# Layer-1 attention of a two-layer transformer kernel: where sums, inverses, additions and minima stand

## The reference

```python
xn = layer_norm(x, ln_gamma, ln_beta)
q, k, v = heads(xn @ Wq), heads(xn @ Wk), heads(xn @ Wv)
att = jnp.einsum('bhid,bhjd->bhij', q, k) / DIM_HEAD ** 0.5
att = att + alibi_bias(S, N_HEADS)[None]
p = jax.nn.softmax(att, axis=-1)
out = jnp.einsum('bhij,bhjd->bhid', p, v)
out = out.transpose(0, 2, 1, 3).reshape(B, S, INNER)
return out @ Wo
```

## Time and profile before

| what | value |
|---|---|
| median of 3 runs | 2318.41 us (2315.52 to 2321.29) |
| profiled execution, its own time | 2305.89 us |
| its span | 2304.0 us |
| granted TensorE clock, mean | 0.985 |
| TensorE, VectorE, GpSimd, ScalarE busy | 95%, 79%, 1385.3 us (60%), 1234.0 us (54%) |
| layer-1 attention | its maxima (line 1034) start from 372.4 to 1906.4 us |

### The profile page before, as it was taken

How to read it: one execution, slowest core, us unless ns; L and a number is a source line. 1 busy time by engine, 2 the same in 40 slices (tenths; PEclk the granted TensorE clock), 3 DMA queues, 4 the chain that set the end, 5 groups by cost and what they waited for, 6 DMA issues and landing times. The chain is left out here.

```text
span 2304.0 us, 40435 instructions
## 1 busy us (share of the span) xinstructions
PE 2197.2 (95%) x10494; PEld 1381.0 (60%) x10531; DVE 1829.4 (79%) x4804; ACT 1234.0 (54%) x1664; POOL 1385.3 (60%) x751
## 2 busy tenths in 40 slices
PE   7989998899999999999999999999999999989995
PEld 4656665456565565656556565655556564449884
DVE  7788886788888888888888888888888887765555
ACT  2232323466666566666656666666666664444442
POOL 2112120578787787878778787887878787643331
PEclk9999999999999999999999999999999999999997
DMA  7050202000000100000100000010000000311114
GB/s 241 22 197 1 85 8 96 21 19 14 16 13 16 35 16 14 13 18 17 34 13 13 21 14 16 13 34 17 14 16 13 20 9 8 148 46 48 46 45 135
DMA packets 90230, 91.25 MB, mean 40 GB/s; under 512 B 22212, under 2 KB 74948, under 8 KB 90120
## 3 DMA queue, kind: packets, MB, share of 16 engines
q1 hardware_dynamic: 85800, 81.35, 11.4%
q0 software_dynamic: 4352, 8.99, 1.2%
HBM read 57.37 MB, written 36.33 MB: 41 GB/s over the span
## 5 line engine op out<-in xcount | busy, mean ns | idle before, releaser
L1624 ACT ACTIVATE big<-P 128x1024 f32<-128x1024 f32 x512 | 512.1, 1020 | 109.2 <-PE P L1993 85.5
L2007 PE MATMUL P<-big,V 128*64 128x512 f32 x2048 | 468.8, 599 | 1.0 <-ACT big L1630 1.0
L649 POOL TENSOR_TENSOR spair<-spair,big 128x1024 f32<-128x1024 f32 x192 | 457.4, 2382 | 15.9 <-DVE hp L810 1.3
L649 POOL TENSOR_TENSOR opair<-opair,big 128x1024 f32<-128x1024 f32 x192 | 457.3, 2382 | 15.0
L1031 DVE CUSTOM_DVE_ANT_0 big<-P,near 128x512 f32<-128x512 f32 x512 | 348.8, 681 | 112.2 <-PE P L1977 108.4
L1977 PE MATMUL P<-kq 96*128 96x512 f32 x1008 | 415.5, 433 | 14.2 <-DVE kq L1015 11.1
L1992 PE MATMUL P<-kq 97*128 97x512 f32 x1024 | 411.4, 402 | 5.7 <-issue 2.8
L1034 DVE TENSOR_REDUCE mhalf<-P 128x1 f32<-128x512 f32 x512 | 349.2, 682 | 79.0 <-PE P L1977 68.5
L1993 PE MATMUL P<-kq 128*128 128x512 f32 x1024 | 408.9, 399 | 0.0
L1977 PEld LDWEIGHTS P<-kq 96*128 96x128 f32 x1008 | 181.8, 190 | 214.3 <-issue 114.0
L2007 PEld LDWEIGHTS P<-big,V 128*64 128x64 f32 x2048 | 135.2, 136 | 265.0 <-issue 262.7
(11 more groups left out here) (316 smaller groups left out, 3663.1 us busy)
## 6 DMA issues: line engine op xcount, KB each, us to landing
slots<-later SPq DMA_DIRECT2D x4, 4224.0 KB, 15.5
kq<-auxrows SPq DMA_DIRECT2D x64, 128.0 KB, 2.3
big<-in_wex SPq DMA_DIRECT2D x8, 768.0 KB, 11.4
xt<-slots SPq DMA_DIRECT2D x76, 66.0 KB, 1.8
near<-in_aux SPq DMA_DIRECT2D x64, 64.0 KB, 1.8
big<-yrows SPq DMA_DIRECT2D x8, 512.0 KB, 7.2
wqk_hi<-wparts SPq DMA_DIRECT2D x62, 64.0 KB, 1.8
wqk_lo<-wparts SPq DMA_DIRECT2D x62, 64.0 KB, 1.9
```

The source lines that it names most:

```text
L649: pool.tensor_tensor(psum8[s][:, :], psum8[s][:, :], pfull[:, j % RING, :], ALU.add).then_inc(S["p_added"], 1)
L1624: act.activation(pfull[:, j, :], banks(2 * (j % 2)), ACT.Exp, scale=DH1 ** -0.5).then_inc(S["exp_done"], 1)
L2007: mm = pe.matmul(P[64 * i:64 * i + 64, 4, :], V1[:, j, s, :], half(pfull[:, j, :], i), start=(j == 0), stop=(j == T - 1))
```

## The change

Six edits. (1) The sum of head n moves from the middle of head n + 1 to behind head n's last V product; it waits for all of GpSimd's additions of head n. (2) ScalarE copies the sums at the start of the next head, and the first half of `turned_out` moves from the end of a head to behind the next head's first exponential. (3) The inverse of heads 1 to 61, and head 0, goes by transfers: two DMAs spread one row of 512 sums each over 64 partitions of 8 columns, VectorE inverts the 128x8 tile, one DMA writes it to DRAM, and two read it back to all partitions. (4) GpSimd scales the head before only behind its seventh addition. (5) In odd heads the output projection's halves move from behind (1,1) and (3,0) to behind (3,0) and (4,0), and VectorE's additions from behind (1,1) and bias 4 to behind bias 4 and (5,0). (6) The minima are joined by a reduction with one input. The waits of bank 5 follow the new order. At the program's start semaphores are merged.

```diff
+            def invert_sums(n, s):
+                at = (lambda v: v) if isinstance(n, int) else sp.snap
+                sp.wait_ge(S["s_copied"], at(n + 1))
+                sp.sem_inc(G["passed"], 1)
+                for i in range(NHALF):
+                    sp.dma_start(rec[64 * i:64 * i + 64, :], sinv[s][64 * i:64 * i + 1, :].rearrange("o (c e) -> o c e", e=N // 128)).then_inc(S["r_in"], 16)
+                sp.wait_ge(S["r_inv"], at(n + 1))
+                sp.sem_inc(G["passed"], 1)
+                sp.dma_start(invd[s].rearrange("i (c e) -> (i c) e", e=N // 128), rec[:, :]).then_inc(S["r_out"], 16)
+                sp.wait_ge(S["r_out"], at(16 * n + 16))
+                sp.sem_inc(G["passed"], 1)
+                for i in range(NHALF):
+                    sp.dma_start(sinv[s][64 * i:64 * i + 64, :], invd[s, i].partition_broadcast(64)).then_inc(S["s_inv"], S_IN)
...
# SP, next_pair: behind load_qk, and behind load_max(2p + 1)
+                if behind:
+                    invert_sums(at(2 * p - 1), 1)
...
+                invert_sums(at(2 * p), 0)
...
# GpSimd, add_head
-                    if behind and j == T - 2:
-                        scaled_out(1 - s, n - 1)
...
+                if behind:
+                    scaled_out(1 - s, n - 1)
...
# GpSimd, last_pairs: the parts of x behind all additions of the head
-                add_head(1, 2 * p + 1, True, range(1, T - 2))
-                scaled_out(0, 2 * p)
+                add_head(1, 2 * p + 1)
...
-                add_head(1, 2 * p + 1, False, range(T - 2, T))
...
# VectorE
+            def invert_rows(n):
+                dve.wait_ge(S["r_in"], NHALF * 16 * (n + 1))
+                if not isinstance(n, int):
+                    dve.sem_inc(G["passed"], 1)
+                dve.reciprocal(rec[:, :], rec[:, :]).then_inc(S["r_inv"], 1)
...
-                    dve.tensor_tensor(mneg[:, b::4], mhalf[rows, 0, :], mhalf[rows, 1, :], ALU.min).then_inc(S["max_both"], 1)
+                    dve.tensor_reduce(mneg[:, b::4], mhalf[rows, :, :].rearrange("p i t -> p t i"), AX.X, ALU.min).then_inc(S["max_both"], 1)
...
# VectorE, head
-                maxima((1, 1))
-                if out:
-                    add_out(p - 1, 0)
-                maxima((2, 0))
+                maxima((1, 1), (2, 0))
                 bias(s, n, 2)
                 maxima((2, 1))
                 bias(s, n, 3)
+                if behind == 2:
+                    invert_rows(n - 1)
                 maxima((3, 0), (3, 1))
                 bias(s, n, 4)
                 if out:
-                    add_out(p - 1, 1)
+                    add_out(p - 1, 0)
                 maxima((4, 0))
                 bias(s, n, 5)
                 maxima((4, 1), (5, 0))
-                if behind:
-                    invert(o, n - 1, 0)
+                if out:
+                    add_out(p - 1, 1)
                 maxima((5, 1), (6, 0))
...
# ScalarE, head
+                if behind == 2:
+                    sums(o, n - 1)
                 exps(n, 0)
+                if behind == 2:
+                    turned_out(s, n - 2, p - 1, 0)
                 exps(n, 1)
...
# TensorE, head
                 maxima((1, 1))
                 if s == 0:
                     project_v(p, 0)
-                if out:
-                    if ahead:
-                        pe.wait_ge(S["q_lo"], 2 * n + 4)
-                        pe.wait_ge(S["k_lo"], 2 * n + 4)
-                    else:
-                        pe.wait_ge(S["s_copied"], n - 1)
-                    out_proj(p - 1, 0)
                 maxima((2, 0))
                 scores(s, n, 2)
                 maxima((2, 1))
                 scores(s, n, 3)
                 maxima((3, 0))
                 if out:
-                    out_proj(p - 1, 1)
+                    pe.wait_ge(S["s_copied"], n)
+                    out_proj(p - 1, 0)
                 if s == 0:
                     project_v(p, 1)
                 maxima((3, 1))
                 scores(s, n, 4)
                 maxima((4, 0))
+                if out:
+                    out_proj(p - 1, 1)
                 scores(s, n, 5)
                 maxima((4, 1))
-                if behind:
...
+                if behind == 1:
+                    pe.wait_ge(S["q_lo"], 2 * n + 4)
+                    pe.wait_ge(S["k_lo"], 2 * n + 4)
                     sum_head(o, n - 1)
                 maxima((5, 0))
...
+                for j in range(3, T):
+                    weigh(s, n, p, j)
+                if ahead == 2:
+                    pe.wait_ge(S["q_lo"], 2 * n + 6)
+                    pe.wait_ge(S["k_lo"], 2 * n + 6)
+                else:
+                    pe.wait_ge(S["v_in"], 2 * p + 2)
+                sum_head(s, n)
...
# TensorE, project_qk, first half: the new predecessors in bank 5
                     if s == 0:
                         pe.wait_ge(S["h_part_ok"], n)
-                    if not isinstance(n, int) or n > 2:
-                        pe.wait_ge(S["s_copied"], n - 2)
+                        pe.wait_ge(S["v_in"], n)
...
+                    else:
+                        pe.wait_ge(S["x_added"], n - 3 + X_AT)
```

More of the change, by code:

```diff
@@ L49 @@
 NINV = 4
+S_IN = 16
 MODS = 6
@@ L188, in network @@
     wparts = nc.dram_tensor("wparts", [2, H1, 128, 2 * DH1], F32).ap()
+    invd = nc.dram_tensor("invd", [2, NHALF, HALF], F32).ap()
     ctx = ExitStack()
@@ L293, in network @@
         kvs = opair[:, 0:D + H0]
+        rec = sb("rec", [128, N // 128])
         mhalf = sb("mhalf", [128, NHALF, T])
@@ L497, in _, with next_pair @@
             sp.wait_ge(G["h_kept"], 16 * B + 16)
-            def next_pair(p, g, new_batch=None, qk=True):
+            def next_pair(p, g, new_batch=None, qk=True, behind=True):
                 at = (lambda v: v) if isinstance(p, int) else sp.snap
@@ L533, in next_pair @@
                 load_max(at(2 * p + 2), 0)
-            next_pair(0, 2, qk=False)
+            next_pair(0, 2, qk=False, behind=False)
             with sp.Fori(1, PAIRS - 1) as q:
@@ L544, in _ @@
                 next_pair((B - 1) * PAIRS + q, 2 * q + 2)
+            invert_sums(HEADS - 3, 1)
             load_max(HEADS - 1, 1)
@@ L741, in _ @@
             add_head(0, HEADS - 2)
-            add_head(1, HEADS - 1, True, range(1, 4))
+            add_head(1, HEADS - 1, False, range(1, 4))
             inverse_root("d0")
@@ L918, in _ @@
             first_norm(h, x0, 1, "f_h")
-            dve.wait_ge(G["mod_spread"], 1)
+            dve.wait_ge(G["mod_mm"], 1)
             dve.wait_ge(S["f_h"], T)
@@ L934, in _ @@
             dve.wait_ge(G["mod_abs"], 3)
[L935 to L938, removed]
+            dve.tensor_scalar(tmp, tmp, 0.25, None, ALU.max).then_inc(G["mod_abs"], 1)
+            dve.wait_ge(G["mod_abs"], 4)
+            dve.scalar_tensor_tensor(gs, sg, -1.0, tmp, ALU.add, ALU.mult).then_inc(G["mod_abs"], 1)
+            dve.wait_ge(G["mod_abs"], 5)
             dve.tensor_scalar(r3[:, 1::3, :], r3[:, 1::3, :], 1.0, None, ALU.add).then_inc(G["mod_one"], 1)
@@ L1004, in invert @@
                 cols = slice(c * HALF // NINV, (c + 1) * HALF // NINV)
-                dve.reciprocal(sinv[s][:, cols], sinv[s][:, cols]).then_inc(S["s_inv"], 1)
+                dve.reciprocal(sinv[s][:, cols], sinv[s][:, cols]).then_inc(S["s_inv"], NHALF * S_IN // NINV)
             def add_out(m, i, bank=5):
@@ L1098, in head @@
                     max_rows(n + 1)
-                if behind:
-                    invert(o, n - 1, 2)
+                if behind == 1:
+                    invert_rows(n - 1)
                 if ahead == 2:
@@ L1665, in head @@
                     k_high(s, n + 2, 1)
-                if ahead == 2:
                     q_again(s, n + 2)
-                if behind:
-                    turned_out(o, n - 1, p - 1 if s == 0 else p, 0)
             act.sem_inc(S["exp_done"], EXP_AT)
@@ L1766, in route_exp @@
                 act.activation(rexp[:, :, 0:E1], rlog[:, :, 0:E1], ACT.Exp).then_inc(S["rd_exp"], 1)
+            sums(0, HEADS - 2)
             exps(HEADS - 1, 0)
+            turned_out(1, HEADS - 3, ALL_PAIRS - 2, 0)
             exps(HEADS - 1, 1)
             turned_out(1, HEADS - 3, ALL_PAIRS - 2, 1)
-            for j in range(2, 5):
+            for j in range(2, 6):
                 exps(HEADS - 1, j)
-            sums(0, HEADS - 2)
-            exps(HEADS - 1, 5)
             outputs(0, HEADS - 2)
@@ L1855, in _ @@
             pe.wait_ge(G["c_silu"], 1)
-            pe.matmul(P[:, 4, 0:2 * D], csb, wmod[:, 0:2 * D], start=True, stop=True).then_inc(G["mod_spread"], 1)
+            pe.matmul(P[:, 4, 0:2 * D], csb, wmod[:, 0:2 * D], start=True, stop=True).then_inc(G["mod_mm"], 1)
             pe.wait_ge(G["c_silu"], 2)
@@ L1935, in project_qk @@
                         pe.wait_ge(S["h_part_ok"], n)
-                    if not isinstance(n, int) or n > 2:
-                        pe.wait_ge(S["s_copied"], n - 2)
-                    elif n == 2:
```

(11 more changed lines are left out.)

28 lines of the change are left out of this document (10 added, 18 removed).

## The result

| | before | after |
|---|---|---|
| median | 2317.36 us (4 runs) | 2375.19 us (2368.5 to 2377.87, 4 runs) |
| ratio | | 1.024 (95% interval 1.022 to 1.026) |
| profiled execution: own time, span | 2305.89, 2304.0 us | 2377.87, 2376.0 us |

The change makes the kernel 58 us slower; the forecast was 38 slower. On a second chip the same kernel took 2355.82 us against 2302.0, so 54 us slower, ratio 1.0241 (1.0221 to 1.0261).

A forecast was written before the change was run, and what follows sets the result against it. The prediction took TensorE, never idle in the steady state, as the bound. Its terms, 56 - 3 - 16 + 2 - 1 = +38 us on 2305.9, gave 2344, and with the 12.5 us offset 2356 us; range 2322 to 2392.

The forecast's parts named there:

- Part 1: Sum behind the last V product instead of mid-head: 0.86 us instead of 1.20, gain 0.34 us a head.
- Part 2: Even heads: sum at head's end nearly ties with GpSimd's additions; -0.1 us a head, -3 us over 31 heads.
- A: Odd heads: TensorE waits for the first half's addition ahead of the second output projection half, 0.66 us.
- B: Odd heads: project_qk waits for the second half's addition, behind maxima (4,1) and (5,0), 0.95 us.
- C: Odd heads: scores 2 and 3 wait for the exponentials, 0.3 us each, 0.6 together; t0 is the head's first maximum.
- Part 4: Edges: GpSimd's extra passes at changes of batch now fit, so the 16 us lost there go: -16 us.
- Start: Head 1: extra sum (+0.86) and aux rows and maxima behind the inverse's transfers (about 1 us): +2 us together.
- Part 5: Costed at nothing: inverse by transfers landing in time, small reciprocal, renamed semaphores, one-input minima not held up.
- 1 (no waits, 36 us faster): Rival: the odd heads' waits do not come, TensorE only gains; 2282 us, chance 0.15.
- 2 (the clock): Rival: granted clock falls at the new waits, once in each odd head, +36 us; 2392 us, chance 0.07.
- 3 (late transfers): Rival: the inverse's transfers land late, VectorE waits 1.7 us in 60 heads, +100 us; 2456 us, chance 0.06.
- 5: Rival: one-input minima are held up by GpSimd too, 60 x 1.6 = +96 us; 2452 us, chance 0.03.

The follow-up runs named there:

- experiment 4: Changed kernel with output projection halves and additions at old places, first turned copy ahead of first exponential: 2274.19 us, ratio 0.9887; rerun on another chip 2272.4 us.
- experiment 9: Kernel before with only the minima joined by a one-input reduction: 2285.3 us, ratio 0.9932.
- experiment 5: Changed kernel run again unchanged, on the second chip: 2355.82 us, ratio 1.0241.
- experiment 3: Changed kernel with both output projection additions earlier on VectorE and the first turned copy ahead of the first exponential: 2282.04 us, ratio 0.9923.
- experiment 7: Changed kernel with the minima joined by the two-input operation again: 2547.63 us, ratio 1.1109.
- experiment 8: Kernel of experiment 4 with inverses made by VectorE in four parts, without transfers of sums: 2275.32 us, ratio 0.9893.

## Why the prediction was right, and where not

The direction and the mechanism were right: moving work off VectorE was worth nothing, and the projection pieces, moved for the sums' sake, wait for additions that now come too late. By its steps:

- **Part 1, sums.** Right in kind, a little high: a gain of 0.34 us predicted for each head, and experiment 4, with the projection in its old places, gains 0.54 a pair, 0.31 in an even head (23.12 for 23.43) and 0.23 in an odd one (23.20).
- **Part 2, even heads.** Right: 23.31 us, predicted 23.33. The sum there waits for GpSimd's last addition, as this row of the changed kernel shows (the bracket is the weight loads' idle time):

```profile
1030.00 0.20 PEld L2039 LDWEIGHTS P<-opair,ones 128*64 128x64 f32 x4 [0.84 <-POOL opair L669]
```

- **A.** 0.66 predicted, 0.65 measured at its place.
- **B.** 0.95 predicted, 1.08 measured. The addition ends 3.51 us behind the start of scores 5, predicted 3.5. What was left out is the hand-over: TensorE starts 0.15 us behind VectorE's end (1044.97 to 1045.12).
- **C.** 0.6 predicted, 0.88 measured: 0.35 ahead of scores 2, 0.53 ahead of scores 3. This is the mis-sized term. The first exponential ends at t0 + 3.57 as counted, but with hand-over scores 2 start at 3.62, and the chain of ScalarE (1.03, 0.63, 1.02 us with 0.02 to 0.03 between) puts the second exponential's end at t0 + 5.27, not 5.1.
- Small intervals around the moved pieces, not counted, add 0.08. An odd head costs 0.65 + 1.08 + 0.88 + 0.08 - 0.34 = +2.35, and the pairs say +2.26 + 0.12 = +2.38; predicted was +1.87. That is +0.5 x 30 = 15 us of the 20 that the forecast was short.
- **The remaining 5 us.** On the second chip the loss is 54 us, 52.4 of it in the 30 pairs. The 4 us more on the first chip may lie in the scatter stretch, but only one execution of each kernel there has a trace, so that is not shown.
- **Part 4, edges.** The number was right (-16), the reason was not. That it came out is luck. I put the lost time down to GpSimd's lack of room for its passes at a change of batch, and let it vanish with the stops. Experiment 9 keeps the stops and loses 14.4 of the 16 us: it was the two-input minimum that was held. The longest minimum of 2272 ns and the waits for the low part of k were both in the rows, and I priced them in different parts of the sum.
- **Start, +2.** The wait for aux rows behind the transfers is there, 2.0 us, and pair 0 is 0.9 longer than before (0.1 in experiment 5). But against experiment 9, with the minima alike, it is about 5 us: edit 6 hid the difference.
- **Part 5.** Right: no wait of VectorE for the rows of sums. A reciprocal of 128x8 takes 0.19 us, and the pieces of 32 bytes land in 1.7 us (below), as long as those of 128 bytes in the earlier trace rows. The Trainium skill ("DMA: Bandwidth & Descriptors", Specifications) speaks against pieces below 512 bytes; at 2 KB a transfer no cost shows.

The transfers of the changed kernel, 380 to 2000 us (count, KB each, median us from issue to landing):

```profile
sinv<-invd SPq DMA_DIRECT2D x124, 128.0 KB, 2.8
...
rec<-sinv SPq DMA_DIRECT2D x124, 2.0 KB, 1.7
...
invd<-rec SPq DMA_DIRECT2D x62, 4.0 KB, 1.4
```

- **The range.** The ends of the terms add up to 0 and +71, so to 2318 and 2389 where the text has 2319 and 2392; nothing hangs on it.

The rivals: 1 (no waits, 36 us faster) did not come; with the idle time of the three waits taken away (experiment 3) the gain is 18 us, half of that. Scores 2 still wait 0.3 us in each odd head, a sum's new place gives less than 0.34, and pair 0 gives back what edit 6 gains there. 2 (the clock) fell: 1.00 in the steady state with waits of 0.3 to 0.8 us. 3 (late transfers) fell, as did 4 (C was larger, not absent). 5 fell, and experiment 7 shows its price had it come: 192 us, not 96: 59 waits of 2.4 us on average, up to 3.5, where I had 1.6.

## What to carry to other kernels

An engine's busy time says nothing about the instruction that a bank waits for: when a producer is moved in one engine's hand-written order, count where the consumer's instruction then stands in the other's, and add the hand-over. Moving one addition ahead of three instructions was worth 31 us in the 30 pairs here; taking 176 us of work off the same engine was worth 3 (experiments 4 and 8). A short instruction with a long maximum among its durations is worth a look on its own: the change of one input gave 17 us with nothing else touched. And a wait need not show as idle time: 0.3 us of C stood in longer intervals only, and the weight loads' own waits show it.

## What the runs showed of the hardware

- A VectorE operation with two inputs in SBUF that starts inside a GpSimd addition is held until the addition ends (experiment 7: 159 ns free, up to 2278 ns; 154 held, all ending 0.02 to 0.03 us behind the addition); a reduction with one input is not, in 222 that start inside an addition (at most 167 ns). This is what the Trainium skill ("SBUF — State Buffer", Who interferes with whom) states, its half on tensor_reduce included, which the trace of before could not show.
- In the odd head shown, from the end of an instruction to the start of the matmul that waits for it are 0.05 us (ScalarE, twice) and 0.13 and 0.15 us (VectorE), and the next interval is longer by about 0.1 (0.07 at B, 0.11 at C).
- One stretch of straight-line code took 98.9 to 102.0 us in ten traces and 118.7 in one, at 0.93 granted clock instead of 0.97 to 1.00; in the one trace with the loads spaced out it took 112.4, at 0.94. The cause is open.
